# A decoder's last stage in three products of rounded parts, with two row tiles ahead of the low-rank part

## What is computed

```python
def _L1_ffn_ref(x, weight, bias, lora_A, lora_B, lora_start_indices):
    y = jnp.einsum('bsd,od->bso', x, weight) + bias
    ...
    A = lora_A[adapter_idx]
    Bw = lora_B[adapter_idx]
    lo = jnp.einsum('bsr,bor->bso', jnp.einsum('bsd,brd->bsr', x, A), Bw) * LORA_SCALE
    use_lora = (seg > 0)[:, None, None]
    return y + jnp.where(use_lora, lo, jnp.zeros((), dtype=y.dtype))
```

## Time and profile before

| | |
|---|---|
| time, median of 3 runs | 1468.35 us (1467.91 to 1472.45) |
| profiled execution | 1467.15 us, its span 1465.0 us |
| PE busy | 1407.8 us, 96% |
| DVE busy | 1090.4 us, 74% |
| ACT busy | 854.6 us, 58% |
| POOL busy | 604.5 us, 41% |
| chain that ended last | PE 53%, DVE 17%, issue 16%, POOL 8%, ACT 4% |
| mean granted clock of PE | 0.991 of full speed |

### The profile page before, as it was taken

How to read it: one execution, slowest core, us unless ns; L and a number is a source line. 1 busy time by engine, 2 the same in 40 slices (tenths; PEclk the granted TensorE clock), 3 DMA queues, 4 the chain that set the end, 5 groups by cost and what they waited for, 6 DMA issues and landing times.

```text
span 1465.0 us, 24269 instructions
## 1 busy us (share of the span) xinstructions
PE 1407.8 (96%) x7610; PEld 1167.8 (80%) x7610; DVE 1090.4 (74%) x2485; ACT 854.6 (58%) x2146; POOL 604.5 (41%) x633
## 2 busy tenths in 40 slices
PE   7999999999989989999999999879999999999997
PEld 6788888887778867787778778668888888888873
DVE  5697667697688877767776776767788788788884
ACT  4556555655223157656755755648677677677660
POOL 4555444444022137556655745435243243242110
PEclk9999999999999999999999999999999999999999
DMA  8011110102122341330321321310111022012000
GB/s 323 1 73 72 73 63 9 72 33 102 58 87 87 114 135 55 103 128 30 130 100 47 111 101 58 129 73 30 40 63 73 15 73 86 15 72 78 1 0 29
DMA packets 30133, 107.72 MB, mean 74 GB/s; under 512 B 3847, under 2 KB 13191, under 8 KB 22104
## 3 DMA queue, kind: packets, MB, share of 16 engines
q1 hardware_dynamic: 30040, 106.58, 20.1%
HBM read 97.07 MB, written 9.50 MB: 73 GB/s over the span
## 4 chain that ended last, share of the span: by engine, by line
PE 53%; DVE 17%; issue 16%; POOL 8%; ACT 4%; DMA 1%; POOLq 0%; DVEq 0%; SPq 0%; ACTq 0%
PE bank L186 11%; PE bank L187 10%; PE bank L188 10%; PE bank L1774 3%; POOL yss L1407 2%; PE bank L316 2%; PE bank L1789 2%; PE bank L339 2%; PE bank L1795 2%; PE bank L1791 2%; POOL tmp L159 1%; PE bank L1231 1%; PE bank L1732 1%; PE bank L327 1%; PE bank L285 1%
## 5 line engine op out<-in xcount | busy, mean ns | idle before, releaser
L159 POOL TENSOR_TENSOR tmp<-tmp,sin 128x512 f32<-128x512 f32 x80 | 111.5, 1394 | 211.2 <-ACT tmp L152 211.2
L188 PE MATMUL bank<-wo_low,att_high 128*128 128x512 f32 x384 | 150.7, 392 | 0.0
L2073 DVE SCALAR_TENSOR_TENSOR logit<-bank,qss,amask 128x512 f32<-128x512 f32 x128 | 90.9, 747 | 57.0 <-PE bank L188 55.9
L1986 POOL TENSOR_TENSOR qss<-qss,half 128x4 f32<-128x4 f32 x32 | 34.9, 1090 | 199.6 <-DVE qss L2059 199.6
L1607 PE MATMUL bank<-kT,wg 128*128 128x256 f32 x512 | 113.1, 383 | 4.0 <-ACT prob L1641 4.0
L1893 ACT ACTIVATE prob<-logit,rmax 128x512 f32<-128x512 f32 x128 | 91.6, 719 | 37.8 <-DVE rmax L2077 37.8
L1607 PEld LDWEIGHTS bank<-kT,wg 128*128 128x128 f32 x512 | 98.1, 192 | 17.9 <-ACT prob L1641 4.4
L186 PE MATMUL bank<-l_wo_high,att_high 128*128 128x512 f32 x256 | 104.7, 409 | 1.8 <-DVE att_low L1491 1.1
L187 PE MATMUL bank<-xT_high,wq_low 128*128 128x512 f32 x256 | 102.3, 400 | 0.0
L187 PE MATMUL bank<-l_wo_high,att_low 128*128 128x512 f32 x256 | 99.8, 390 | 0.0
L1907 ACT ACTIVATE p_high<-bank 128x512 fp32r<-128x512 f32 x128 | 70.1, 597 | 46.4 <-PE bank L1774 46.1
(11 more groups left out here) (270 smaller groups left out, 4414.1 us busy)
## 6 DMA issues: line engine op xcount, KB each, us to landing
wq<-in_l_wq SPq DMA_DIRECT2D x16, 1024.0 KB, 6.6
wo<-in_l_wo SPq DMA_DIRECT2D x16, 1024.0 KB, 5.0
wkv<-in_l_wkv SPq DMA_DIRECT2D x16, 512.0 KB, 5.7
wg<-in_l_wg SPq DMA_DIRECT2D x8, 1024.0 KB, 4.8
wq<-in_x_wq SPq DMA_DIRECT2D x8, 1024.0 KB, 7.2
wo<-in_x_wo SPq DMA_DIRECT2D x8, 1024.0 KB, 4.9
kT<-in_x_wkv SPq DMA_DIRECT2D x8, 512.0 KB, 4.2
kv_keys<-logit SPq DMA_DIRECT2D x8, 512.0 KB, 4.6
```

What stands on the lines that cost most here:

```text
L159: eng.tensor_tensor(halves(tmp[4 + j % 2]), halves(tmp[2 + j % 2]), per_batch(sin), ALU.mult).then_inc(sem(f"{l}_sinp"), 1)
L188: return eng.matmul(dst, a_high, b_low, start=False, stop=stop)
L2073: dve.scalar_tensor_tensor(logit[s % 2][:, c, :], bank[3 + c][:, :], qss[p][:, 1, h, 2 * b + c:2 * b + c + 1], amask[:, c, :], ALU.mult, A ...
```

## The change

It has four parts.

1. **Split weights.** In the last group of the cross attention ScalarE copies the feed-forward weights, two chunks in step 6 and two in step 7, and the low-rank matrix (128x192) in step 7, rounded, each time between `normalise` and `headed`. GpSimd subtracts, behind the last output-projection weights.
2. **The last stage as rounded products.** Norm 4 writes `xT_high`, and VectorE makes `xT_low`: tile 0 ahead of the normalisation of tiles 2 and 3, tile 1 behind it, tiles 2 and 3 at the start of `ffn_vector`. `whole` has twelve matmuls instead of four f32 products (eight records), the four that need `xT_low` last; `low_rank` twelve instead of four.
3. **Order on TensorE.** whole(0), whole(1), transposes of tiles 2 and 3, low_rank(0), low_rank(1), whole(2), added(0), added(1), added(2), whole(3), added(3). whole(t) waits for its own transposed tile only.
4. **Last norm.** Tiles 2 and 3 get statistics, power and normalisation one by one. VectorE's order is: both selections, adds 0 and 1, norm of these two, add 2, statistics 2, add 3, statistics 3, rows 2, rows 3.

Besides, the four semaphores of the Sinkhorn start are merged into two, and `dt_turn` is counted on `dt`.

```diff
+        def ln_split_tile(dve, n, t):
+            dve.wait_ge(sem("ln_xT"), NT * n + t + 1)
+            cols = slice(t * P, (t + 1) * P)
+            dve.tensor_tensor(xT_low[:, :, cols],
+                              turn_bank(n, t)[:, :].rearrange("p (c t) -> p c t", c=KC),
+                              xT_high[:, :, cols].bitcast(F32), ALU.subtract).then_inc(sem("low_part"), 1)
+
+        def last_stats(dve, t):
+            seen = 2 * NT * 5 + 2 * t
+            dve.wait_ge(sem("rows_added"), NT + t + 1)
+            dve.bn_stats(stat[:, t, :], x[:, t, :]).then_inc(sem("ln_stat"), 1)
+            dve.wait_ge(sem("ln_stat"), seen + 1)
+            dve.bn_aggr(mv[:, t, :], stat[:, t, :]).then_inc(sem("ln_stat"), 1)
+            dve.wait_ge(sem("ln_stat"), seen + 2)
+            dve.tensor_scalar(lnr[:, 0, t:t + 1], mv[:, t, 1:2], LN_EPS, None, ALU.add).then_inc(sem("ln_var"), 1)
+
+        def last_row(dve, t):
+            dve.wait_ge(sem("ln_rstd"), 2 * 5 + t)
+            dve.tensor_scalar(x[:, t, :], x[:, t, :], mv[:, t, 0:1], lnr[:, 1, t:t + 1],
+                              ALU.subtract, ALU.mult).then_inc(sem("ln_x"), 1)
...
+                    if s in (6, 7) and last_group:
+                        act.wait_ge(sem("ld_ffn"), 16 * 5)
+                        for c in (2 * s - 12, 2 * s - 11):
+                            high_chunk(act, "ffn_high", wq_high[0], wq[0], c)
+                        if s == 7:
+                            act.activation(lora_high[:, :, :], loraA[:, :, :], ACT.Copy).then_inc(sem("ffn_high"), 1)
...
+                if last_group:
+                    for c in range(KC):
+                        pool.wait_ge(sem("ffn_high"), c + 1)
+                        low_chunk(pool, "ffn_low", wq_high[0], wq_low[0], wq[0], c)
+                    pool.wait_ge(sem("ffn_high"), KC + 1)
+                    pool.tensor_tensor(lora_low[:, :, :], loraA[:, :, :], lora_high[:, :, :].bitcast(F32),
+                                       ALU.subtract).then_inc(sem("ffn_low"), 1)
...
                     ln_stats(dve, 4, 1, "x_added", 4 * g)
+                    ln_split_tile(dve, 4, 0)
                     ln_rows(dve, 4, 1)
+                    ln_split_tile(dve, 4, 1)
...
             def low_rank(k):
-                pe.wait_ge(sem("ln_xT"), NT * 4 + 2 * k + 2)
+                pe.wait_ge(sem("low_part"), FFN_LOW + 2 * k + 2)
+                pe.wait_ge(sem("ffn_low"), KC + 1)
+                cols = slice(k * L, (k + 1) * L)
                 for c in range(KC):
-                    last = pe.matmul(bank[LOW_BANKS[k]][0:NR, 0:L], loraA[:, c, :], xT[:, c, k * L:(k + 1) * L],
-                                     start=(c == 0), stop=(c == KC - 1))
+                    last = product(pe, bank[LOW_BANKS[k]][0:NR, 0:L], (lora_high[:, c, :], lora_low[:, c, :]),
+                                   (xT_high[:, c, cols], xT_low[:, c, cols]), c == 0, c == KC - 1)
                 last.then_inc(sem("lora"), 1)
 
             def whole(t):
+                cols = slice(t * P, (t + 1) * P)
+                pe.wait_ge(sem("ln_xT"), NT * 4 + t + 1)
                 for c in range(KC):
-                    pe.matmul(bank[OUT_BANKS[t]][:, :], xT[:, c, t * P:(t + 1) * P], wq[0][:, c, :],
+                    if t == 0:
+                        pe.wait_ge(sem("ffn_low"), c + 1)
+                    pe.matmul(bank[OUT_BANKS[t]][:, :], xT_high[:, c, cols], wq_high[0][:, c, :],
                               start=(c == 0), stop=False)
+                    pe.matmul(bank[OUT_BANKS[t]][:, :], xT_high[:, c, cols], wq_low[0][:, c, :],
+                              start=False, stop=False)
+                pe.wait_ge(sem("low_part"), FFN_LOW + t + 1)
+                for c in range(KC):
+                    pe.matmul(bank[OUT_BANKS[t]][:, :], xT_low[:, c, cols], wq_high[0][:, c, :],
+                              start=False, stop=False)
...
-            pe.wait_ge(sem("ld_ffn"), 16 * 5)
             pe.wait_ge(sem("x_added"), 4 * NG)
+            whole(0)
+            whole(1)
+            ln_tensor(pe, 4, 1)
             low_rank(0)
-            whole(0)
-            ln_tensor(pe, 4, 1)
-            added(0)
-            whole(1)
-            added(1)
             low_rank(1)
-            for t in PAIRS[1]:
-                whole(t)
+            whole(2)
+            for t in range(3):
                 added(t)
+            whole(3)
+            added(3)
...
+            ln_split(dve, 4, 1)
             selected(0)
+            selected(1)
             add(0)
             add(1)
-            selected(1)
             ln_stats(dve, 5, 0, "rows_added", NT)
             ln_rows(dve, 5, 0)
-            add(2)
-            add(3)
-            ln_stats(dve, 5, 1, "rows_added", NT)
-            ln_rows(dve, 5, 1)
+            for t in PAIRS[1]:
+                add(t)
+                last_stats(dve, t)
+            for t in PAIRS[1]:
+                last_row(dve, t)
```

More of the change, by code:

```diff
@@ L700, in ln_split, with last_power @@
             for t in PAIRS[k]:
[L701 to L705, removed]
+                ln_split_tile(dve, n, t)
+        def ln_split_tile(dve, n, t):
[16 more added lines that the diff above has]
+                              ALU.subtract, ALU.mult).then_inc(sem("ln_x"), 1)
+        def last_power(pool, t):
+            pool.wait_ge(sem("ln_var"), 2 * 5 + t)
+            pool.tensor_tensor(lnr[:, 1, t:t + 1], lnr[:, 0, t:t + 1], half[:, 0:1], ALU.pow)\
+                .then_inc(sem("ln_rstd"), 1)
         def ln_scalar(act, n, k, high=None):
@@ L845, in mix_vector @@
                 step(dve, dve.tensor_reduce(vec4(mx), lines, AX.X, ALU.max))
-                dve.tensor_tensor(t4, src, wide(mx), ALU.subtract).then_inc(sem("sink_in"), 1)
-                dve.wait_ge(sem("sink_exp"), side + 1)
+                dve.tensor_tensor(t4, src, wide(mx), ALU.subtract).then_inc(sem("sink_vector"), 1)
+                dve.wait_ge(sem("sink_scalar"), 2 * side + 1)
                 t_lines = t4 if side == 0 else rows4(ztmp[:, :, :], True)
-                dve.tensor_reduce(vec4(zsm[:, 2, :]), t_lines, AX.X, ALU.add).then_inc(sem("sink_sum"), 1)
-                dve.wait_ge(sem("sink_ln"), side + 1)
+                dve.tensor_reduce(vec4(zsm[:, 2, :]), t_lines, AX.X, ALU.add).then_inc(sem("sink_vector"), 1)
+                dve.wait_ge(sem("sink_scalar"), 2 * side + 2)
                 step(dve, dve.tensor_tensor(ls, ls, mx, ALU.add))
@@ L975, in sink_scalar @@
             for side in range(2):
[L976 to L979, removed]
+                act.wait_ge(sem("sink_vector"), 2 * side + 1)
+                act.activation(z, z, ACT.Exp).then_inc(sem("sink_scalar"), 1)
+                act.wait_ge(sem("sink_vector"), 2 * side + 2)
+                act.activation(zsm[:, 1, :], zsm[:, 2, :], ACT.Ln).then_inc(sem("sink_scalar"), 1)
             act.wait_ge(sem("mix_ready"), 1)
@@ L1083, in dt_turn @@
                 last = pe.transpose(bank[5][:, n * 32:(n + 1) * 32], src[:, at:at + P], ident[0:32, 0:32])
-            last.then_inc(sem("dt_turn"), 1)
+            last.then_inc(sem("dt"), 1)
         def dt_scalar(act):
@@ L1382, in l1_scalar @@
             value(0, 0, bank[4])
-            act.wait_ge(sem("dt_turn"), 1)
+            act.wait_ge(sem("dt"), 2)
             act.activation(cols[:, :, :].rearrange("p a b -> p (a b)"), bank[5][:, 0:320], ACT.Copy)\
@@ L2323, in _ @@
             for k in range(2):
-                ln_scalar(act, 4, k)
+                ln_scalar(act, 4, k, xT_high)
         @block.gpsimd
@@ L2345, in _ @@
             for n in (4, 5):
-                for k in range(2):
+                for k in range(2 if n == 4 else 1):
                     ln_gpsimd(pool, n, k)
+            for t in PAIRS[1]:
+                last_power(pool, t)
         @block.tensor
```

3 lines of the change are left out of this document (added).

## The result

Over 14 runs each on the same chip, the changed kernel took 1466.81 us (median; 1463.66 to 1471.28) and the kernel before 1471.62 us (1467.47 to 1475.23). The prediction, 1465.0 on a median of 1468.35, is a ratio of 0.9977. The measured 0.29% lies just inside the 0.3% that the prediction called no change, and its interval reaches to both sides of it.

A forecast was written before the change was run, and what follows sets the result against it. TensorE's matmuls bound the last stage, then an uncovered VectorE and GpSimd tail. Tail -4.24, ScalarE copies +1.08 and stores -0.2 sum to -3.4 us: 1465.0 from a median of 1468.35, range 1462.3 to 1468.0.

The forecast's parts named there:

- Part 1: ScalarE's weight copies ahead of the last head copy: TensorE's projection and all behind it 1.08 us later.
- Part 2: First two tiles: TensorE starts 0.48 us sooner, 2.79 us per tile; VectorE's two new remainder steps cost nothing.
- Part 3: Second-pair transposes to last addition on TensorE: 0.2 us stall before second low-rank product; last addition starts 1452.9 against 1457.07.
- Part 4: Last norm: VectorE reaches the last addition 0.8 us late; last power 0.93 us; last row ends 4.24 us sooner.
- Part 5: Final stores: the first goes out with 0.8 us of lead, so the end comes 0.2 us sooner.
- It hides more: ScalarE's scaling and VectorE's last stretch cost less than summed: 1463.9 or 1463.1 us; chance 0.22.
- The clock falls in the tail: TensorE's added idling drops its clock to 1.2 GHz in the last stage: +15 us, 1483; chance 0.04.
- The rounded products gain nothing: Last stage: three rounded matmuls take as long as two full-precision records: about +0.6 us, 1469.0; chance 0.05.
- outside the stage: New layout of code and semaphores, beyond the last stage: within 1.5 us either way; chance 0.07.

The follow-up runs named there:

- the pair norm: Changed kernel with the last norm of tiles 2 and 3 again as a pair; 34.98 us from last softmax scaling to last row step, against 34.96.
- the plain reordered kernel: Kernel before with TensorE's new order, both selections up front and single-tile last norm, but plain f32 products; 1467.76 us, ratio 0.9986.
- The three mends with the copies behind the head copy: Changed kernel with ScalarE's weight copies behind the head copy, VectorE's tile 2 addition earlier, TensorE's tile 2 before second low-rank product; 1464.07 us, ratio 0.9949.
- the other order of rows: Changed kernel with row step and store of tile 3 ahead of tile 2; 35.20 us from last softmax scaling to last row step, against 34.96.
- the last experiment: Changed kernel with early weight copies, tile 2 moves on VectorE and TensorE, and GpSimd's later two remainders held until step 6's scaling; 1463.94 us in one run.

## Why the prediction was right

All its steps can be laid on the trace of after, by taking off the 3.92 us by which that profile is later, and from tile 0 on the 1.11 us of part 1 as well.

| step | predicted | after |
|---|---|---|
| head copy | 1425.99 | 1426.04 |
| delay of part 1 | +1.08 | +1.11 |
| tile 0 starts | 1434.35 | 1434.30 |
| tile 0 ends | 1437.15 | 1437.15 |
| tile 1 ends | 1439.95 | 1439.94 |
| second low-rank product | 1442.6 | 1442.62 |
| tile 2 starts | 1444.1 | 1444.06 |
| additions start | 1447.1 | 1446.92 |
| tile 3 starts | 1449.9 | 1449.69 |
| last addition, TensorE | 1452.9 | 1452.68 |
| last addition, VectorE | 1454.8 | 1454.70 |
| last power | 0.93 | 0.79 |
| last row ends | 1458.1 | 1457.97 |
| stores | -0.2 | -0.23 |

*Part 1* held to 0.05 us. That price lay in two lines of the earlier trace rows and one habit: ask what an added instruction stands in front of on its own engine. The size taken for the 192-column copy, 0.20, came out as 0.25 between starts (1429.71 to 1429.96).

*Part 2* held, and its cover with it, the first of VectorE's two new steps only just: it ended at 1441.09, the weight load that reads it waited 0.15 us for it, and the matmul behind that load still started at its usual distance (1441.04 to 1441.27). TensorE's matmuls show no stall inside the first two tiles. The rounded matmul cost 0.233 us in the new place as in the old. The Trainium skill's formula ("TensorE: Matmul & The Clock Gate", section on the back-to-back issue gap) would have made it 0.216. But that section of the Trainium skill gives the formula for an isolated gap; for a stream in which each matmul has its own weight load, as here, it states about 131 ns at 512 columns. The runs show neither: the starts inside the tiles of after lie 0.23 to 0.24 apart.

*Part 3* held to 0.2 us. The stall ahead of the second low-rank product came, for the reason given, but was 0.40 us and not 0.2: TensorE was done with the first product 0.2 us sooner than summed, and the second started on time. From the additions on the trace is 0.2 us ahead of the sum, which counted one change of weights twice. Its 0.19 us is what a tile pays for both changes, to 49 rows and back; in the trace of after they are 0.09 and 0.10 us (the last matmul of tile 2 starts 0.32 us ahead of the additions, the first gap of tile 3 is 0.34, against 0.23).

*Part 4*, the least certain, was right on its main point: VectorE and not TensorE is last. TensorE could have been served 0.82 us sooner, as the pair norm shows, and the experiment that moved the addition of tile 2 got those 0.82 back. The forecast had said 0.8. The power's price was wrong in its base and right in its surcharge. A power for one tile takes 0.55 us alone where I used the two-tile 0.70; beside a row step it takes 0.24 more, where I had read 0.23 from the earlier trace rows.

*Part 5*: 0.23 instead of 0.2.

The sum by the traces is 3.5 us, and 3.4 was forecast. Of the measured 4.3 (2.6 to 5.9 by the interval) the other 0.8 us is inside the scatter of the clock; the second set of the same kernel gave 3.8. What the prediction had wrong is its range's working, not its sum: "scatter between median and profile 1" should have been some 4 us either way. The kernel before had shown 1467.91 to 1472.45 in three runs, which said as much. On 14 runs its median was 1471.62, so that the absolute 1466.81 lies 1.8 us above the forecast while the difference is 0.9 us larger than forecast. That 1466.81 lies inside the range of 1462.3 to 1468.0 is in part luck: the forecast ratio on the median of 14 runs would have given 1468.2, outside it. I also expected a span near 1461.6. A span of 1465.4 with the same steps comes from the stretch between 900 and 1020 us and its lower granted clock, which the distance from a fixed line takes out.

*The rivals.* "It hides more" fell: the delay of part 1 and VectorE's lateness are both there at full size, and each was got back only by an edit. "The clock falls in the tail" fell: the granted clock is 1.00 from 1420 to 1458 us, also behind the 1.0 us wait of TensorE at 1430.93. "The rounded products gain nothing" fell, with the plain reordered kernel 1.43 us longer in the closing distance. Of "outside the stage", nothing shows beyond the scatter; the loss between 900 and 1020 us also met the plain reordered kernel (3.3 us), whose instructions there are those of the kernel before.

**The better version.** The three mends with the copies behind the head copy beat both kernels by the closing distance, which is 2.35 us shorter than the changed kernel's. By the ratio to the kernel before it is 0.51% (0.30 to 0.71) faster, where the changed kernel had 0.29 and 0.26; these intervals overlap, so the times alone do not show the step over the changed kernel. Its sum by the traces is 3.5 + 2.35 = 5.9 us, 0.40%; the rest of the 0.51 is not explained by the stage and may be scatter, since the interval holds 0.40.

## What to carry to other kernels

Price a new instruction by what it stands in front of, on its own engine (here 1.1 us for three copies ahead of one that feeds TensorE) and what it runs beside on another engine (0.67 us lost where GpSimd's subtractions ran beside VectorE's scaling). When the bounding engine gets faster, follow the next engine's queue up to the same instant before booking the gain: of 3.15 us that rounding saved on TensorE, 2.5 arrived, and 1.1 of these went to ScalarE's copies. Where a run's time scatters by more than the effect, measure from a fixed instruction ahead of the change to the last one: that distance repeated to 0.01 us while the spans differed by 2.3.

## What the hardware showed that was not expected

*A subtraction on GpSimd can hold a scalar step of VectorE for more than a microsecond; a power need not.* The 128x512 scaling of scores took 1.62 us instead of 0.49 beside GpSimd's 128x512 subtractions of 1.27 us each; with the subtractions moved it took 0.49 again. The Trainium skill ("SBUF — State Buffer", section on the two separate sides) says that the two engines share a port pair, locked for a whole instruction, and this trace agrees for the subtraction: the scaling, started at 1424.34, ended 0.28 us behind the last subtraction (1425.96, 1425.68), although that one started only at 1424.4, after it. The kernel before had shown it already: a smaller scaling (L570, two shapes) takes 0.35 us in the median and 1.38 us at most, beside such subtractions near 357 us.

For a power the traces do not bear this section of the Trainium skill out. By it, whichever starts first has the ports for its whole length, and the other waits. But the same scaling kept its 0.49 us when it ran inside a GpSimd power that had begun before it and lasted 1.64 us; this is the kernel before, and the profiles before and after have seven such places each:

```profile
1008.05 1.64 POOL L1980 TENSOR_TENSOR kss<-kss,half 128x8 f32<-128x8 f32 x1 [1.33 <-DVE kss L2033]
1008.22 0.49 DVE L2084 TENSOR_SCALAR prob<-prob,rsum 128x512 f32<-128x512 f32 x1
```

In the other order, a power started beside a running row step, the row step kept its 0.54 us, and the power grew by 0.24 us (0.79, 1461.62 in after) where 0.38 us of the row step were left, and by 0.32 beside two row steps in a row (0.87, 1460.67 in the experiment with the moved addition). Which part of a power waits, no run here shows.

*The run's time goes with the clock granted in one stretch in the middle.* The 14 runs of after go from 1463.66 us at a mean granted clock of 0.992 to 1471.28 at 0.981. In the profiles, the last scaling starts anywhere from 1424.12 to 1431.70 us. The three earliest (before, the pair norm, the other order of rows: 1424.12 to 1425.05) all have a clock of 0.97 in the window 900 to 1000 and 1.00 in 1000 to 1100; the seven latest (1428.04 and on) have 0.89 to 0.93 and 0.97 to 0.98; the last experiment, at 1427.06, lies between with 0.93 and 1.00. Laid on before's profile by VectorE's starts, the ten others are 0.7 us ahead to 2.7 behind at 900 us, and 0.4 to 7.6 behind from 1020 us; from there to 1418 us none of these distances moves by more than 0.1 us. Apart from the first 20 us TensorE is at its idlest in this stretch, 14.6 of 20 us busy from 960 to 980 in before's profile. Why one execution gets the clock back and the next doesn't, no run here tells. Nor is it shown that the change has no part in how often that happens: two of the nine profiles of changed kernels kept the clock there, against one of before and none of the plain reordered kernel.
